# A decoder block in one kernel: the first row's queries, keys and first scores in front of the second row's work, the output weights split on GpSimd, and the statistics of the other rows further on

## The chip, the cores and the metric

One core of one Trainium2 chip runs the whole kernel. The metric is the time of one execution on the device in microseconds (us); lower is better. TensorE (PE) multiplies and transposes, VectorE (DVE) and ScalarE (ACT) work on PSUM and SBUF, GpSimd (POOL) works on SBUF alone, and SyncE (SP) only issues transfers. Every engine runs its own instruction list strictly in order; semaphores join the lists.

## The reference

`x` is 8 rows (batch entries) of 128 tokens by 512 features. Three blocks follow each other, each with a residual: self-attention, cross-attention to a context, and a linear layer with 4-bit weights. The change touches only the self-attention, cut here to what matters:

```python
x = x + _L0_attn_ref(_layernorm(x), Wq, Wk, Wv, Wo)       # changed part
x = x + _L0_xattn_ref(_layernorm(x), ctx_4096, ...)        # most of the time
x = x + _L0_ffn_ref(_layernorm(x), weight_q4, weight_scale, bias)

def _L0_attn_ref(h, Wq, Wk, Wv, Wo):                       # H=32 heads of 16, 8 key heads
    q, k, v = heads(h @ Wq.T), heads(h @ Wk.T), heads(h @ Wv.T)
    qr, kr = apply_rope(q, cos, sin), apply_rope(k, cos, sin)
    scores = einsum('bhqd,bhkd->bhqk', qr, kr) / 4 + causal_mask
    return einsum('bhqk,bhkd->bhqd', softmax(scores), v) @ Wo.T
```

## The kernel before

**Precision.** Products run on fp32 data split in two: a high part, rounded to the matmul format by a copy, and a low part, which is the rest. A product is three matmuls (high·high, low·high, high·low), `split_matmuls`, line 69. So each operand costs a copy (mostly ACT) and a subtraction (DVE or POOL).

**Rows.** The self-attention handles the 8 rows one by one; row n's work is overlapped with the preparation of rows n+1 and n+2. Four hand-written instruction lists, one per engine, have the form of a loop over `n` from -1 (the prologue) on. Nothing is scheduled by a planner: the order in the code is the order on the engine. Lines with `if n == -1` are the prologue.

**A row's steps.**
- `statistics` (DVE, lines 658 and 661) and `rstd_1` (POOL, 329 and 331) give mean and inverse deviation, `normalised` (DVE, 544) the normalised row, `xn_transposed` (PE, 777) its transpose, `xn_high` (ACT, 435) and `xn_low` (DVE, 549) the two parts.
- The projections (PE, line 74) give queries and keys/values. For row 1 the query projection is `second_row_queries`, two halves of six matmuls into `a_ps_o`, placed by hand in the prologue.
- `rope_queries` and `rope_keys` (DVE, 559 to 561) and `rotate_queries` and `rotate_keys` (POOL, 359 to 370) rotate them; `queries_high` (ACT, 442) and `queries_low` (DVE, 593) split the queries. Row 0's queries go in two halves of 16 heads.
- `query_tiles` and `key_tiles` transpose on PE (818, 827) and copy out (ACT 447 and 452, DVE 600).
- `scores(n, k)` for six units k (PE, 842 to 849) alternates between two PSUM banks, `ps_kv` and `ps_q`; `maxima` (DVE, 605), `exps` (ACT, 461), `probs_transposed` (PE 860, copied out by DVE 611) follow. `scores(n, k)` needs the exponentials of unit k-2.
- `inverse_totals` (DVE, 615 and 618) turns the softmax sums into a wide tile that PE transposes (904); `values` (PE, 876 and 884) and `project_output` (PE, line 74 into `a_ps_w`) close the row.

**Output weights.** `a_wo` is loaded into `raw_qo`; ACT makes the high part (line 495), POOL the low part (line 400). The first user is `project_output(0)`.

The cross-attention begins when all engines are through with the self-attention.

Of the kernel before, what the change touches and what calls it, by code (L numbers as in the profile page):

```python
# [28 lines left out]
G = H // KVH  # L29
# [162 lines left out]
def self_attention(nc, mem, io):  # L192
# [12 lines left out]
    with ExitStack() as ctx:  # L205
# [114 lines left out]
        def _(pool):  # L320
# [74 lines left out]
            rstd_1(2, slice(2, 4))  # L395

            def output_weights_low():
# [8 lines left out]
            for m in range(1, B + 2):  # L406
                if m < B:
                    rotate_keys(m)
                if m == 1:
                    rstd_1(3, slice(4, 6))  # L410
                if m < B:
                    rotate_queries(m)
                if m <= B:
                    if m < B:
                        pool.wait_ge(q_lo, m + 2)
                    context(m - 1)
                if m == 1:
                    output_weights_low()
                    rstd_1(4, slice(6, B))
# [12 lines left out]
        def _(act):  # L432
# [56 lines left out]
            for n in range(-1, B + 1):  # L489
                now, after = 0 <= n < B, n + 1 < B  # L490
                if n == -1:
                    xn_high(1)
                    queries_high(0, 0)
                    act.wait_ge(wo_in, 16)
                    act.activation(wo[0][:], raw_qo[:], ACT.Copy).then_inc(wo_hi, 1)
                    queries_high(0, 1)
                elif after:
                    queries_high(n + 1)
# [6 lines left out]
                if n == -1:  # L505
                    key_tiles(0)
                if after:
                    query_tiles(n + 1, 0)
                if after and now:
                    key_tiles(n + 1)  # L510
# [4 lines left out]
                if n == -1:  # L515
                    exps(0, 0)
# [23 lines left out]
        def _(dve):  # L540
# [137 lines left out]
            statistics(range(1, 2))  # L678
            normalised(1)
            dve.wait_ge(tab_in, 32)  # L680
            for n in range(-1, B + 1):
                now, after, later = 0 <= n < B, n + 1 < B, n + 2 < B
                if n == -1:
                    rope_queries(0, 0)
                    rope_keys(0)
                    xn_low(1)
                    pad_values(0)
                    queries_low(0, 0)
                    rope_queries(0, 1)
                elif after and now and n > 0:  # L690
                    rope_queries(n + 1)
# [16 lines left out]
                if n == -1:  # L708
                    dve.wait_ge(x_in, 16)
                    statistics(range(2, 4))  # L710
                    queries_low(0, 1)
                if after:
# [14 lines left out]
                if n == 0:  # L727
                    statistics(range(6, B))
# [5 lines left out]
                if later:  # L734
                    rope_keys(n + 2)
                if n == -1:
                    pad_values(1)
                    maxima(0, 0)
                    maxima(0, 1)
# [10 lines left out]
                if n == -1:  # L750
                    rope_queries(1)
# [6 lines left out]
                if after:  # L758
                    maxima(n + 1, 2)
                if n == -1:  # L760
                    statistics(range(4, 6))
# [7 lines left out]
        def _(pe):  # L769
# [177 lines left out]
            for i in range(WARM_UP // 4):  # L947
                pe.transpose(ps_s[1][:, 0:P], ident[:], ident[:])
            project_keys_values(1)
            pe.wait_ge(consts, 2)  # L950
            for n in range(-1, B):
# [9 lines left out]
                if after:  # L961
# [4 lines left out]
                if after:  # L966
                    query_tiles(n + 1, 0)
                if n == -1:
                    query_tiles(0, 1)
                    second_row_queries(0)  # L970
                    scores(0, 0)
                    scores(0, 1)
                    second_row_queries(1)
                    query_tiles(0, 2)
# [25 lines left out]
                if later and now:  # L1000
                    project_queries(n + 2)
                if after:
                    scores(n + 1, 2)
# [695 lines left out]
```

## Time and profile before

| | |
|---|---|
| median of 3 runs | 947.81 us (946.51 to 948.13) |
| the profiled execution | 946.93 us |
| its span, first to last instruction | 945.2 us |
| PE busy | 915.2 us, 97% of the span |
| DVE, ACT, POOL busy | 726.0, 607.4, 566.9 us |
| granted TensorE clock, mean | 0.994 of full |
| prologue (until the first scores) | about 22 us |
| self-attention ends on PE | about 190 us |

PE's share is an average over stages. The prologue and the first row look different from the rest, so the question is read there, instruction by instruction. A row of the timeline gives the start, the duration, the engine, the line, what was written and read, and in square brackets how long the engine had been idle and who released it. Consecutive instructions of one engine overlap a little, so an instruction starts up to 0.1 us before its predecessor's row ends.

### The profile page before, as it was taken

The page shows a single profiled execution, that of the slowest core. Times are in us where ns is not written, and L with a number is a line of the kernel's source. Part 1 is how long each engine was busy: PE and PEld are TensorE (multiplying, and loading weights), DVE is VectorE, ACT ScalarE, POOL GpSimd, SP SyncE. Part 2 cuts the span into 40 slices and gives each one's busy share as a digit, 9 for nine tenths or more (in the row PEclk, how much of TensorE's full clock was granted, in tenths as well). Part 3 has the DMA queues.
Part 4 walks back from the last instruction along what each step waited for, and adds up shares of the span by engine and source line. Part 5 has one row for each costly group of instructions (what it writes and reads, how often), then busy time and mean ns, then how long its engine had stood idle before and what let it go on. Part 6 is the DMA issues. An engine that isn't in the chain of part 4 may idle for free.

```text
span 945.2 us, 17557 instructions
## 1 busy us (share of the span) xinstructions
PE 915.2 (97%) x5496; PEld 788.4 (83%) x5504; DVE 726.0 (77%) x1559; ACT 607.4 (64%) x2230; POOL 566.9 (60%) x600
## 2 busy tenths in 40 slices
PE   8899998989999999999999999999999999999987
PEld 7677776778888888888888888888888888888776
DVE  7788888667777777777777777777777777789985
ACT  4788887557566756666666567666755675665540
POOL 7532323349656855685578557646865686468742
PEclk9999999999999999999999999999999999999999
DMA  5000120166665666566557655665566556654431
GB/s 213 12 12 13 24 79 12 34 220 218 208 213 165 194 212 205 156 218 203 177 170 232 207 172 172 224 202 156 180 219 212 164 167 212 217 170 150 141 128 57
DMA packets 101164, 149.84 MB, mean 159 GB/s; under 512 B 11856, under 2 KB 77392, under 8 KB 98896
## 3 DMA queue, kind: packets, MB, share of 16 engines
q1 hardware_dynamic: 101072, 148.71, 49.3%
q8 instruction: 45, 0.74, 0.3%
q14 instruction: 47, 0.39, 0.1%
HBM read 87.85 MB, written 60.82 MB: 157 GB/s over the span
## 4 chain that ended last, share of the span: by engine, by line
PE 69%; DVE 4%; POOL 3%; ACT 2%; DMA 1%; issue 1%; SPq 0%; DVEq 0%; POOLq 0%
PE ps_q L74 17%; PE ps_kv L74 17%; PE ps_y L74 17%; PE ps_s L74 8%; PE ps_o L74 8%; POOL wo_lo L1186 1%; POOL pT_raw L1198 1%; ACT ps_s L1273 1%; PE ps_f L74 1%; DMA raw_wkv<-in_x_wkv 1%; DVE neg_max L1352 0%; DVE p L1364 0%; POOL qT_lo L1191 0%; DVE p_blocks L1368 0%; DVE x L1379 0%
## 5 line engine op out<-in xcount | busy, mean ns | idle before, releaser
L1273 ACT ACTIVATE ps_s<-ps_s,bias,q_rms 128x256 f32<-128x256 f32 x256 | 136.6, 534 | 138.2 <-DVE bias L1356 138.2
L1191 POOL TENSOR_TENSOR qT_lo<-qk_raw,qT_hi 128x512 fp32r<-128x512 f32 x64 | 84.8, 1325 | 201.9 <-ACT qT_hi L1285 201.9
L1198 POOL TENSOR_TENSOR pT_raw<-pT_raw,pT_hi_sb 128x1024 fp32r<-128x1024 f32 x63 | 151.7, 2408 | 6.0 <-ACT pT_hi_sb L1279 5.6
L125 ACT ACTIVATE q_squares<-ps_q 128x128 bf16<-128x128 f32 x256 | 67.4, 277 | 109.7 <-DVE qk_blocks L151 109.7
L74 PE MATMUL ps_y<-wo_hi,oT_hi 128*128 128x512 f32 x252 | 99.7, 395 | 4.0 <-DVE oT_lo L1383 4.0
L74 PE MATMUL ps_q<-wq_hi,xT_hi 128*128 128x512 f32 x256 | 101.3, 396 | 0.7 <-PEq L205 0.7
L74 PE MATMUL ps_q<-wq_lo,xT_hi 128*128 128x512 f32 x256 | 101.5, 396 | 0.0
L1368 DVE STREAM_TRANSPOSE p_blocks<-p 128x512 f32<-128x512 f32 x128 | 91.1, 712 | 13.3
L74 PE MATMUL ps_q<-wq_hi,xT_lo 128*128 128x512 f32 x256 | 101.0, 395 | 0.0
L74 PE MATMUL ps_y<-wo_hi,oT_lo 128*128 128x512 f32 x252 | 99.3, 394 | 0.0
L74 PE MATMUL ps_y<-wo_lo,oT_hi 128*128 128x512 f32 x252 | 99.0, 393 | 0.0
L1379 DVE TENSOR_TENSOR x<-ps_y,x 128x512 f32<-128x512 f32 x64 | 44.2, 690 | 66.2 <-PE ps_y L74 65.4
L1364 DVE TENSOR_TENSOR p<-ps_s,inv 128x512 f32<-128x512 f32 x128 | 88.5, 691 | 4.4
L1352 DVE TENSOR_REDUCE neg_max<-ps_s 128x2 f32<-128x512 f32 x128 | 87.6, 684 | 4.9
L151 DVE STREAM_TRANSPOSE qk_blocks<-ps_q 128x512 f32<-128x512 f32 x64 | 45.8, 715 | 41.2 <-PE ps_q L74 41.1
L74 PE MATMUL ps_s<-kT_hi,qT_hi 128*128 128x256 f32 x256 | 72.6, 284 | 3.2 <-DVE kT_lo L1372 2.2
L74 PE MATMUL ps_s<-kT_hi,qT_lo 128*128 128x256 f32 x256 | 72.7, 284 | 0.0
L74 PE MATMUL ps_s<-kT_lo,qT_hi 128*128 128x256 f32 x256 | 72.6, 284 | 0.0
L74 PE MATMUL ps_kv<-wkv_hi,cT_hi 128*128 128x256 f32 x256 | 72.4, 283 | 0.0
L74 PE MATMUL ps_kv<-wkv_hi,cT_lo 128*128 128x256 f32 x256 | 72.2, 282 | 0.0
L74 PE MATMUL ps_kv<-wkv_hi,xT_lo 128*128 128x256 f32 x256 | 71.9, 281 | 0.0
L74 PE MATMUL ps_kv<-wkv_hi,xT_hi 128*128 128x256 f32 x256 | 71.9, 281 | 0.0
(261 smaller groups left out, 2916.1 us busy)
## 6 DMA issues: line engine op xcount, KB each, us to landing
p_scratch<-p_blocks SPq DMA_DIRECT2D x64, 512.0 KB, 3.0
pT_raw<-p_scratch SPq DMA_DIRECT2D x256, 128.0 KB, 3.0
qk_scratch<-qk_blocks SPq DMA_DIRECT2D x64, 384.0 KB, 3.5
qk_raw<-qk_scratch SPq DMA_DIRECT2D x256, 96.0 KB, 3.0
raw_wq<-in_x_wq SPq DMA_DIRECT2D x8, 1024.0 KB, 7.8
raw_wo<-in_x_wo SPq DMA_DIRECT2D x8, 1024.0 KB, 7.8
raw_wkv<-in_x_wkv SPq DMA_DIRECT2D x8, 512.0 KB, 4.9
ctx_raw<-in_ctxT SPq DMA_DIRECT2D x8, 256.0 KB, 2.6
```

What stands on the lines that cost most here:

```text
L74: mm = pe.matmul(out, lhsT, rhs, start=start and i == 0, stop=stop and i == len(terms) - 1)
L125: i = act.activation(x["q_squares"][:, g, :], x["ps_q"][:, g * XD:(g + 1) * XD], ACT.Square, scale=XD ** -0.5, accum_out=x["q_mean"][:, g: ...
L151: dve.transpose(x["qk_blocks"][:, :, 0:XG, :].rearrange("p j x c -> p x j c"), x["ps_q"][:].rearrange("p (g j r) -> p g j r", g=XG, r=R)). ...
L1186: i = pool.tensor_tensor(w[1][:, c, :], raw[:, c, :], f32(w[0][:, c, :]), ALU.subtract)
L1191: pool.tensor_tensor(qT[1][:].rearrange("p g (i c) -> p g i c", i=4), qk_raw[s % 2][:, :, 0:XG, :].rearrange("p i g c -> p g i c"), f32(qT ...
L1198: pool.tensor_tensor(raw, f32(raw), f32(pT_hi_sb[:].rearrange("p i t x -> p (i t x)")), ALU.subtract).then_inc(pT_lo, 1)
L1273: e = act.activation(scores, scores, ACT.Exp, bias=bias[:, g:g + 1], scale=q_rms[:, s % 4, g:g + 1], accum_out=total[:, g:g + 1])
L1352: dve.tensor_reduce(neg_max[:, two], ps_s[h][:].rearrange("p (g k) -> p g k", g=2), AX.X, ALU.max, negate=True).then_inc(max_ok, 1)
L1364: dve.tensor_tensor(p[:, two, :], ps_s[h][:].rearrange("p (g k) -> p g k", g=2), inv[:, two].unsqueeze(2).broadcast_to([P, 2, KV]), ALU.mu ...
L1368: dve.transpose(p_blocks[:, :, two, :], p[:, two, :].rearrange("p g (m r) -> p m g r", r=R)).then_inc(p_blocked, 1)
L1379: dve.tensor_tensor(acc[:, b, :], ps_y[:], acc[:, b, :], ALU.add).then_inc(acc_ok, 1)
```

## The change

On every engine the list of the prologue is re-ordered, and one step moves to another engine:

- **PE**: row 0's query tiles 0 and 1 and its key tiles go in front of row 1's key/value projection, and `scores(0, 0)` and `scores(0, 1)` right behind it. Query tile 2 and `scores(0, 2)` now stand in front of the second half of row 1's queries.
- **DVE**: row 0's first query half is rotated before row 1 is normalised; its values and query low parts come before `xn_low(1)`; key tiles and maxima follow at once. The statistics of rows 2 and 3 move behind `rope_queries(1)`, those of rows 4 and 5 from the prologue into row 0, next to those of rows 6 and 7, ahead of `inverse_totals(0)`.
- **ACT**: `queries_high(0, 0)` before `xn_high(1)`, key tiles before the second query tile, and the output weights' copy is gone.
- **POOL**: `rstd_1` of rows 2 and 3 stands behind `rotate_queries(1)`, that of rows 4 and 5 behind the output weights, of which POOL now does the high part too, in four copies.

```diff
 # POOL
+            def output_weights():
+                pool.wait_ge(wo_in, 16)
+                for g in range(G):
+                    i = pool.tensor_copy(wo[0][:, g, :], raw_qo[:, g, :])
+                i.then_inc(wo_hi, 1)
                 pool.wait_ge(wo_hi, 1)
                 for g in range(G):
                     i = pool.tensor_tensor(wo[1][:, g, :], raw_qo[:, g, :], f32(wo[0][:, g, :]), ALU.subtract)
...
-                if m == 1:
-                    rstd_1(3, slice(4, 6))
                 if m < B:
                     rotate_queries(m)
+                if m == 1:
+                    rstd_1(2, slice(2, 4))
 # ACT
                 if n == -1:
+                    queries_high(0, 0)
                     xn_high(1)
-                    queries_high(0, 0)
-                    act.wait_ge(wo_in, 16)
-                    act.activation(wo[0][:], raw_qo[:], ACT.Copy).then_inc(wo_hi, 1)
-                    queries_high(0, 1)
 # DVE
                 if n == 0:
+                    statistics(range(4, 6))
                     statistics(range(6, B))
                 if now:
                     inverse_totals(n)
 # PE
+            query_tiles(0, 0)
+            query_tiles(0, 1)
+            key_tiles(0)
             project_keys_values(1)
             pe.wait_ge(consts, 2)
+            scores(0, 0)
+            scores(0, 1)
+            second_row_queries(0)
+            query_tiles(0, 2)
+            scores(0, 2)
+            second_row_queries(1)
```

**PE, from the first scores on.** In these rows `a_ps_o` is the projection of row 1's queries, `ps_kv` and `ps_q` the scores of row 0. Before:

```order
L847 MATMUL ps_kv<-a_kT,a_qT 128x256 x2
L849 MATMUL ps_kv<-mask,ident 128x4x64
L847 MATMUL ps_q<-a_kT,a_qT 128x256 x2
L849 MATMUL ps_q<-mask,ident 128x4x64
L74 MATMUL a_ps_o<-wq_hi,a_xnT_hi 128x512
...
L74 MATMUL a_ps_o<-wq_hi,a_xnT_lo 128x512
L818 MATMUL a_ps_u<-ident,q_stack 128x2x64 x4
L842 MATMUL ps_kv<-a_kT,a_qT 128x128 x4
L844 MATMUL ps_kv<-mask,ident 128x512
L818 MATMUL a_ps_t<-ident,q_stack 128x2x64 x4
L860 MATMUL a_ps_pT<-ident,a_p 128x128 x8
```

And with the change, from query tile 2 (`a_ps_u`) on:

```order
L816 MATMUL a_ps_u<-ident,q_stack 128x2x64 x4
L840 MATMUL ps_kv<-a_kT,a_qT 128x128 x4
L842 MATMUL ps_kv<-mask,ident 128x512
L74 MATMUL a_ps_o<-wq_hi,a_xnT_hi 128x512
...
L74 MATMUL a_ps_o<-wq_hi,a_xnT_lo 128x512
L816 MATMUL a_ps_t<-ident,q_stack 128x2x64 x4
L858 MATMUL a_ps_pT<-ident,a_p 128x128 x8
```

The second half of row 1's queries has gone behind the third unit of scores (four small matmuls and the mask), which waits for the exponentials of unit 0.

**DVE, from the third maxima of row 0 to its fourth.** Here `ps_kv` and `ps_q` are units 2 and 3, and `a_ps_o` is row 1's queries. Before:

```order
L559 TENSOR_TENSOR rot_c<-a_ps_o,cos 128x512
L560 TENSOR_TENSOR rot_s<-a_ps_o,sin 128x32x8
L561 TENSOR_TENSOR rot_s<-a_ps_o,sin 128x32x8
L605 TENSOR_REDUCE a_neg_max<-ps_kv 128x8
L658 BN_STATS a_stats<-x 128x6 x2
L661 BN_AGGR a_moments<-a_stats 128x2 x2
L605 TENSOR_REDUCE a_neg_max<-ps_q 128x4
```

With the change:

```order
L604 TENSOR_REDUCE a_neg_max<-ps_kv 128x8
L558 TENSOR_TENSOR rot_c<-a_ps_o,cos 128x512
L559 TENSOR_TENSOR rot_s<-a_ps_o,sin 128x32x8
L560 TENSOR_TENSOR rot_s<-a_ps_o,sin 128x32x8
L657 BN_STATS a_stats<-x 128x6 x2
L660 BN_AGGR a_moments<-a_stats 128x2 x2
L604 TENSOR_REDUCE a_neg_max<-ps_q 128x4
```

The rotation now comes after the third maxima. A pair of statistics still stands in front of the fourth, but it is that of rows 2 and 3, which before was done in the prologue.

**DVE, the end of row 0**, from its key cast for row 1 to the wide inverse; with the change:

```order
L599 CAST a_kT<-a_ps_w 64x4x128
L604 TENSOR_REDUCE a_neg_max<-ps_q 128x8
L610 COPY a_pT<-a_ps_pT 128x512 x2
L657 BN_STATS a_stats<-x 128x6 x2
L660 BN_AGGR a_moments<-a_stats 128x2 x2
L657 BN_STATS a_stats<-x 128x6 x2
L660 BN_AGGR a_moments<-a_stats 128x2 x2
L614 RECIPROCAL a_inv<-a_total 128x32
L617 COPY a_inv_wide<-a_inv 128x512
```

Before, the same list had one pair of statistics here; now it has two.

## Rows read from the trace of the kernel before

**Rows 1.** The page: PE's and DVE's busy time over the whole span

```profile
PE 915.2 (97%) x5496; PEld 788.4 (83%) x5504; DVE 726.0 (77%) x1559; ACT 607.4 (64%) x2230; POOL 566.9 (60%) x600
```

**Rows 2.** Busy time in three stretches: length, engines (instructions), PE clock, DMA

```profile
26.00:29.60 3.60, 1.68 (x14) 1.21 (x11) 3.57 (x8) 3.52 (x21) 1.44 (x3) 1.00 0.00 0
29.60:33.00 3.40, 3.30 (x14) 2.94 (x15) 3.25 (x5) 2.61 (x10) 0.98 (x2) 0.51 0.00 0
60.00:80.00 20.00, 19.13 (x141) 15.46 (x142) 17.32 (x36) 16.85 (x76) 5.89 (x8) 1.00 0.05 14
```

**Rows 3.** Timeline of PE: start, duration, what; idle time before and releaser

```profile
18.59 0.63 PE L827 MATMUL a_ps_w<-ident,k_stack 128*128 128x128 f32 x4 [0.18 <-issue]
...
21.59 0.47 PE L847 MATMUL ps_kv<-a_kT,a_qT 128*128 128x256 f32 x2
...
22.30 0.48 PE L74 MATMUL a_ps_o<-wq_hi,a_xnT_hi 128*128 128x512 f32 x1
...
23.55 0.39 PE L74 MATMUL a_ps_o<-wq_hi,a_xnT_lo 128*128 128x512 f32 x1
...
24.92 0.63 PE L842 MATMUL ps_kv<-a_kT,a_qT 128*128 128x128 f32 x4 [0.54 <-ACT a_p L461]
25.62 0.60 PE L818 MATMUL a_ps_t<-ident,q_stack 128*128 128x128 f32 x4
...
29.66 0.75 PE L847 MATMUL ps_kv<-a_kT,a_qT 128*128 128x256 f32 x2 [1.93 <-ACT a_p L461]
...
30.69 1.12 PE L777 MATMUL a_ps_t<-ident,a_xn 128*128 128x128 f32 x4
...
41.53 0.63 PE L904 MATMUL a_ps_u<-ident,a_inv_wide 128*128 128x128 f32 x4
...
48.37 0.48 PE L74 MATMUL a_ps_w<-a_wo_hi,a_oT_hi 128*128 128x512 f32 x1
```

**Rows 4.** Timeline of DVE

```profile
13.99 0.55 DVE L544 TENSOR_SCALAR a_xn<-x,a_moments,a_rstd 128x512 f32<-128x512 f32 x1 [1.01 <-POOL a_rstd L331]
...
15.19 0.28 DVE L559 TENSOR_TENSOR rot_c<-a_ps_w,cos 128x128 f32<-128x128 f32 x1
...
23.98 0.69 DVE L559 TENSOR_TENSOR rot_c<-a_ps_o,cos 128x512 f32<-128x512 f32 x1 [0.15 <-PE a_ps_o L74]
...
24.92 0.42 DVE L561 TENSOR_TENSOR rot_s<-a_ps_o,sin 128x256 f32<-128x256 f32 x1
...
29.68 0.96 DVE L544 TENSOR_SCALAR a_xn<-x,a_moments,a_rstd 128x512 f32<-128x512 f32 x1
...
36.62 0.68 DVE L600 CAST a_kT<-a_ps_w 64x512 fp32r<-64x512 f32 x1 [2.56 <-ACT a_kT L452]
...
39.02 1.27 DVE L658 BATCH_NORM_STATS2 a_stats<-x 128x6 f32<-128x512 f32 x2
...
40.48 0.32 DVE L615 RECIPROCAL a_inv<-a_total 128x32 f32<-128x32 f32 x1
40.84 0.43 DVE L618 COPY a_inv_wide<-a_inv 128x512 f32<-128x512 f32 x1
```

**Rows 5.** Timeline of ACT

```profile
16.65 1.90 ACT L495 ACTIVATE a_wo_hi<-raw_wq 128x2048 fp32r<-128x2048 f32 x1
...
30.39 1.06 ACT L442 ACTIVATE q_stack<-rot 128x1024 fp32r<-128x1024 f32 x1 [0.87 <-POOL rot L359]
...
35.53 0.59 ACT L452 ACTIVATE a_kT<-a_ps_w 64x512 fp32r<-64x512 f32 x1
```

**Rows 6.** Timeline of POOL

```profile
17.33 1.16 POOL L370 TENSOR_TENSOR k_stack<-rot,k_stack 128x256 fp32r<-128x256 f32 x1
...
29.08 1.27 POOL L359 TENSOR_TENSOR rot<-rot_c,rot_s 128x512 f32<-128x512 f32 x1
32.77 0.61 POOL L383 CAST cT_hi<-ctx_raw 128x512 fp32r<-128x512 f32 x1 [2.42 <-DVE q_stack L593]
...
34.72 5.00 POOL L400 TENSOR_TENSOR a_wo_lo<-raw_wq,a_wo_hi 128x512 fp32r<-128x512 f32 x4
```

More of the change, by code:

```diff
@@ L417, in _ @@
                 if m == 1:
-                    output_weights_low()
+                    output_weights()
+                    rstd_1(3, slice(4, 6))
                     rstd_1(4, slice(6, B))
@@ L504, in _ @@
                     exps(n, 4)
-                if n == -1:
-                    key_tiles(0)
                 if after:
                     query_tiles(n + 1, 0)
-                if after and now:
                     key_tiles(n + 1)
@@ L515, in _ @@
                 if n == -1:
+                    queries_high(0, 1)
                     exps(0, 0)
@@ L678, in _ @@
             statistics(range(1, 2))
+            dve.wait_ge(tab_in, 32)
+            rope_queries(0, 0)
             normalised(1)
-            dve.wait_ge(tab_in, 32)
             for n in range(-1, B + 1):
@@ L683, in _ @@
                 if n == -1:
-                    rope_queries(0, 0)
                     rope_keys(0)
-                    xn_low(1)
                     pad_values(0)
                     queries_low(0, 0)
+                    xn_low(1)
                     rope_queries(0, 1)
+                    key_tiles(0)
+                    maxima(0, 0)
+                    queries_low(0, 1)
+                    maxima(0, 1)
+                    rope_keys(1)
+                    pad_values(1)
+                    maxima(0, 2)
+                    rope_queries(1)
+                    dve.wait_ge(x_in, 16)
+                    statistics(range(2, 4))
                 elif after and now and n > 0:
@@ L707, in _ @@
                     xn_low(n + 2)
[L708 to L712, printed above, removed]
+                if after and now:
                     key_tiles(n + 1)
@@ L733, in _ @@
                     cross_weights_high(0)
-                if later:
+                if later and now:
                     rope_keys(n + 2)
[L736 to L739, printed above, removed]
                 if after and now:
@@ L757, in _ @@
                     step_queries_blocked(dve, mem, 0)
-                if after:
+                if after and now:
                     maxima(n + 1, 2)
-                if n == -1:
-                    statistics(range(4, 6))
                 if n == B - 2:
@@ L960, in _ @@
                     probs_transposed(n, 2)
-                if after:
+                if after and now:
                     key_tiles(n + 1)
@@ L965, in _ @@
                     probs_transposed(n, 3)
-                if after:
+                if after and now:
                     query_tiles(n + 1, 0)
[L968 to L974, printed above, removed]
                 if now:
@@ L1001, in _ @@
                     project_queries(n + 2)
+                if after and now:
+                    scores(n + 1, 2)
                 if after:
-                    scores(n + 1, 2)
                     query_tiles(n + 1, 3)
```

5 lines of the change are left out of this document (1 added, 4 removed).

## The prediction, made before the changed kernel had run

> **What bounds the kernel now.** I read the page first: PE is busy for 915.2 of 945.2 us [rows 1]. A change in the first 45 us therefore acts by one thing: how much earlier or later PE enters the stretch that it then works through. Next the table of stretches. From 60 to 80 us PE works 19.13 of 20.00 us [rows 2], so in the steady rows it is nearly continuous, and a shift at their entry goes on to the end almost one for one. Between 26.0 and 29.6 us it works only 1.68 of 3.60 us, and in the following 3.40 us it is granted 0.51 of its clock, the level of 1.2 GHz instead of 2.4, while busy for 3.30 us [rows 2]. Last, the timelines. The reader should look for the places where PE waits on the way to the steady stretch: 1.93 us in front of unit 4 of row 0's scores, for exponentials [rows 3]; and for where the chain leaves PE. That is the end of row 0: PE's transpose of the wide inverse starts at 41.53, 0.26 us after DVE finished that tile at 40.84 + 0.43 = 41.27 [rows 3, 4]. From there on PE is at work without a long gap. So the forecast is the new time of one instruction, the end of `a_inv_wide` on DVE, against 41.27.
>
> **Step 1, the first scores, a gain.** DVE waited 1.01 us in front of row 1's normalisation [rows 4]; row 0's first query rotation now fills that hole. The key rotation, which began at 15.19, follows the normalisation directly (13.99 + 0.55 less some overlap, 14.5), 0.7 us earlier. POOL's last key part took 1.16 us [rows 6] and ended at 18.49; moved, it ends 0.7 us earlier, or 1.1 if it also loses what stretched it. Row 1's twelve key/value matmuls no longer stand ahead, so the key transposes go from 18.59 [rows 3] to 17.4 to 17.9. Then come the transposes (0.63), ACT's copy (0.59 [rows 5]), DVE's cast (0.68 [rows 4]) and three hand-overs of about 0.1: 2.2 us. First scores at 19.6 to 20.1 instead of 21.59 [rows 3], 1.5 to 2.0 us earlier. The twelve matmuls lie beside that chain.
>
> ACT's removed copy (1.90 us [rows 5]) helps row 0's second query half here, and nothing else waits for it.
>
> **Step 2, row 1's queries, a loss.** Unit 2 of the scores started at 24.92 after waiting for exponentials [rows 3]. It moves with step 1, and by 0.3 us more because DVE takes up the first maxima at once: 22.6 to 23.1. The second half of row 1's queries used to run from 22.30 to 23.94 (23.55 + 0.39), inside that wait [rows 3]. Now it is queued behind the waiting unit 2: 0.70 us for the unit (24.92 to 25.62) and 1.64 for the half, so the queries are ready at 24.95 to 25.45, 1.0 to 1.5 us **later**. Who waits for them: `rope_queries(1)`, and in DVE's order everything behind it.
>
> **Step 3, DVE until row 2 is normalised.** The rotation took 1.36 us (23.98 to 24.92 + 0.42 [rows 4]), 1.28 before the next starts. Behind it now stands a pair of statistics, 1.46 us (39.02 to 40.48 [rows 4]), then maxima and two copies. For these I take the stretch from the key cast at 36.62 to 39.02, 2.40 us, less the cast's 0.60: 1.80. Start of the normalisation: 25.0 to 25.5, plus 1.28 + 1.46 + 1.80 = 4.54, so 29.5 to 30.0. Before it took 0.96 us from 29.68, while POOL was rotating from 29.08 on [rows 4, 6]; the same operation took 0.55 at 13.99 [rows 4]. POOL is now done by then, so it ends at 30.05 to 30.55 instead of 30.64, and PE's transposes of row 2 start 0.1 to 0.6 us earlier than 30.69 [rows 3]. Of the 1.5 to 2.0 us this is what is left. `rotate_queries(1)` is itself much earlier: POOL no longer holds it until 29.08 behind rows 4 and 5's statistics, so `queries_high(1)` leaves 30.39 [rows 5] by some 2 us. That is off the path, because PE and DVE in order come to their part of it no sooner.
>
> **Step 4, PE's clock.** Before, PE went from the 30.69 transposes to row 1's key tiles at 0.51 clock until 33.0 [rows 2, 3]. With the change its wait in front of unit 4 remains, and a second one, until the normalisation, follows it: in the 3 us ahead of the transposes PE works 0.7 us, less than the 1.68 in 3.60 that preceded the fall before. I expect the fall again, chance 7 in 10. Then the key cast at 36.62 [rows 4] comes at 36.0 to 36.5. It began 0.50 us after ACT's copy had ended (35.53 + 0.59 = 36.12 [rows 5]), which is several times the usual hand-over; if that vanishes, 35.5. So 35.5 to 36.5. Without the fall, half of 30.69 to 33.0 is saved, 1.15 us: 34.4 to 35.4.
>
> **Step 5, the statistics at the end of row 0, a loss.** From the cast, DVE does 2.40 us of maxima and copies, then now two pairs of statistics, 2.92 instead of 1.46, then 0.79 until the wide inverse ends (40.48 to 41.27) [rows 4]: 6.11 in all. Before, the single pair ended just as the sums came. Now the second pair lies bare. The inverse ends at cast + 6.11: 41.6 to 42.6 with the slow stretch, middle 42.1, against 41.27: **0.35 to 1.35 us later**, middle 0.85. Without it 40.5 to 41.5: 0.75 earlier to 0.25 later.
>
> **Step 6, output weights on POOL.** Four casts at 0.61 (a 128x512 cast [rows 6]) are 2.4 us, the low parts 5.00 as before. They started at 34.72, after q-parts of row 1 that come up to 0.5 us earlier now; so they end at 41.6 to 42.2. The first user is PE at 48.37 [rows 3]: 6 us of cover, and nothing on the path. The casts would have to take 2.1 us each before PE waited. What they do is keep POOL busy while DVE makes the wide inverse, a copy within SBUF like the normalisation that went from 0.55 to 0.96 beside POOL: between 0 and 0.4 us on the path. I take 0.1, because POOL may just be through. The later `rstd_1` of rows 4 and 5 delays `rotate_keys(2)` on POOL by about 1 us; its tiles are wanted at some 52 us, so it costs nothing.
>
> The Trainium skill (GPSIMD Engine Reference, section Specifications) says that GpSimd shares its SBUF interfaces with VectorE, with contention for VectorE's two-port modes and for its instructions with two SBUF inputs. By that rule the full 0.4 would be paid; by the row at 40.84, where POOL was free, nothing.
>
> **Sum.** 0.85 + 0.1, rounded to 0.9 us later. Against the profiled execution: span 945.2 + 0.9 = 946.1, and 946.93 + 0.9 = 947.8 with what lies around it. That execution was 0.88 us under the median of the runs shown, so for the median 947.81 + 0.9 = 948.7. About 0.2% (1.9 us) is what a measurement of this kernel can tell from no change, so my answer is: none that can be told.
>
> **The rivals.**
> - *Given back, as above*: +0.0 to +1.9, 948.7 (its own range 947.8 to 949.7). Chance 0.50.
> - *Full clock*: the statistics still lie bare, but PE isn't slowed: -0.75 to +0.65, about 947.8. For it: step 2 puts the query half late, near the wait, and the clock may hold. Chance 0.22.
> - *The gain goes through*: steps 2 and 5 cost nothing, because DVE's 2.56 us of waiting in front of the key cast [rows 4] moves with everything else and leaves room. Then the 1.5 to 2.0 us stay: 946.0. Against it: both pairs are listed behind the cast, not in that hole. Chance 0.13.
> - *Slower*: the clock falls a stretch earlier, at PE's wait for unit 2 or 4, and stays down for a second 3.4 us; PE's work in it costs half as much again in wall time, up to 1.7 us on top: 947.81 + 0.9 + 1.7 = 950.4. It decides if the granted clock is already at half before unit 3's scores. Chance 0.10.
> - *Output weights late*: PE would wait at 48.4 for the low part. It needs 6 us more than worked out. Chance 0.03.
> - The rest, 0.02, is what I don't see.
>
> **How the numbers follow.** The likeliest case gives 948.7. The range takes in the full-clock case, most of the gain that goes through, and the lower half of the slower case: 946.0 to 950.2, with some 0.05 left out below and 0.1 above. Faster by over 0.2% (under 945.9) is only the better part of the third case: 0.09. Slower by over 0.2% (above 949.7) is the fourth, half of the fifth and the tail of the first: 0.14. Between them 0.77.
>
> **What would show it.** In the profile after: first scores at 19.6 to 20.1; unit 2 at about 22.9; `rope_queries(1)` starting at 25.0 to 25.5; a granted clock near 0.5 somewhere between 29 and 34; DVE's four statistics of rows 4 to 7 in one piece, with the reciprocal right behind them and the exponentials of row 0 already done; PE idle for about a microsecond in front of the inverse's transposes, which start at 41.0 to 42.9. The prediction is wrong if DVE reaches the reciprocal before 39, if the clock falls twice, or if PE waits for `a_wo_lo`.

## The result and the profile after

| | before | after |
|---|---|---|
| median, timed alternately on one chip | 947.85 us (946.51 to 948.85, 9 runs) | 949.51 us (947.72 to 951.96, 9 runs) |
| the profiled execution, its span | 946.93, 945.2 | 949.63, 947.9 |
| granted TensorE clock, mean | 0.994 | 0.993 |

The ratio is 1.0022 with a 95% interval of 1.0014 to 1.0031: about 2 us slower, 1.66 by the medians, where 0.9 was forecast. On PE the end of row 0 is 0.90 us late, which is the forecast amount; another 1.5 us are lost right behind it, in a stretch at the lower clock that the forecast had at another place.

The page, PE's and DVE's busy time, answers to [rows 1]. The work is the same but for the step that moved (four instructions more on POOL, one fewer on ACT), so what was lost is waiting or work at a lower clock:

```profile
PE 915.4 (97%) x5496; PEld 788.3 (83%) x5504; DVE 726.8 (77%) x1559; ACT 605.6 (64%) x2229; POOL 567.8 (60%) x604
```

The table of stretches after, columns as in [rows 2], with one stretch more:

```profile
26.00:29.60 3.60, 1.68 (x16) 1.47 (x14) 3.57 (x9) 3.18 (x18) 1.88 (x3) 1.00 0.00 0
29.60:33.00 3.40, 2.44 (x20) 2.21 (x21) 3.40 (x6) 3.35 (x15) 0.48 (x2) 1.00 0.00 0
42.00:47.00 5.00, 4.57 (x22) 2.49 (x23) 3.71 (x11) 3.07 (x13) 3.94 (x8) 0.66 0.00 2
60.00:80.00 20.00, 19.14 (x142) 15.47 (x142) 17.36 (x35) 16.84 (x78) 5.89 (x8) 1.00 0.05 17
```

From 29.6 to 33.0 us the clock is full where it was 0.51 [rows 2]. From 42 to 47 us it is 0.66, and PE there issues 22 matmuls. In the kernel before it issued 33 at full clock:

```profile
42.00:47.00 5.00, 4.93 (x33) 3.50 (x33) 3.46 (x11) 4.02 (x18) 1.88 (x3) 1.00 0.01 3
```

PE's timeline after, beside [rows 3]:

```profile
20.68 0.47 PE L845 MATMUL ps_kv<-a_kT,a_qT 128*128 128x256 f32 x2 [0.25 <-DVE a_kT L599]
...
23.68 0.63 PE L840 MATMUL ps_kv<-a_kT,a_qT 128*128 128x128 f32 x4 [0.22 <-ACT a_p L465]
...
25.55 0.39 PE L74 MATMUL a_ps_o<-wq_hi,a_xnT_lo 128*128 128x512 f32 x1
25.78 0.60 PE L816 MATMUL a_ps_t<-ident,q_stack 128*128 128x128 f32 x4
...
29.54 0.47 PE L845 MATMUL ps_kv<-a_kT,a_qT 128*128 128x256 f32 x2 [1.92 <-ACT a_p L465]
...
31.09 0.66 PE L775 MATMUL a_ps_t<-ident,a_xn 128*128 128x128 f32 x4 [0.96 <-DVE a_xn L543]
...
40.15 0.28 PE L847 MATMUL ps_q<-mask,ident 128*128 128x256 bf16 x1
42.43 0.70 PE L902 MATMUL a_ps_u<-ident,a_inv_wide 128*128 128x128 f32 x4 [2.00 <-DVE a_inv_wide L617]
43.05 1.08 PE L874 MATMUL a_ps_o<-a_pT,a_v_pad 128*32 128x256 f32 x8
```

The first scores start 0.91 us earlier than at 21.59. Unit 4 is only 0.12 us earlier than at 29.66, and the inverse's transposes are 0.90 us later than at 41.53 [rows 3]. In the kernel before, PE came to these transposes straight from its own work, and the eight small matmuls behind them, which take 1.08 us now, took 0.64 at full clock:

```profile
41.30 0.28 PE L849 MATMUL ps_q<-mask,ident 128*128 128x256 bf16 x1
...
42.09 0.64 PE L876 MATMUL a_ps_o<-a_pT,a_v_pad 128*32 128x256 f32 x8
```

DVE's timeline after, beside [rows 4]:

```profile
14.02 0.94 DVE L543 TENSOR_SCALAR a_xn<-x,a_moments,a_rstd 128x512 f32<-128x512 f32 x1 [0.28 <-POOL a_rstd L331]
...
16.00 1.19 DVE L592 TENSOR_TENSOR q_stack<-rot,q_stack 128x512 fp32r<-128x512 f32 x1
...
25.98 0.69 DVE L558 TENSOR_TENSOR rot_c<-a_ps_o,cos 128x512 f32<-128x512 f32 x1 [0.70 <-PE a_ps_o L74]
...
30.50 0.54 DVE L543 TENSOR_SCALAR a_xn<-x,a_moments,a_rstd 128x512 f32<-128x512 f32 x1
...
35.48 0.68 DVE L599 CAST a_kT<-a_ps_w 64x512 fp32r<-64x512 f32 x1 [1.51 <-ACT a_kT L456]
...
39.34 1.25 DVE L657 BATCH_NORM_STATS2 a_stats<-x 128x6 f32<-128x512 f32 x2
...
40.80 0.32 DVE L614 RECIPROCAL a_inv<-a_total 128x32 f32<-128x32 f32 x1
41.15 1.22 DVE L617 COPY a_inv_wide<-a_inv 128x512 f32<-128x512 f32 x1
```

The wide copy took 1.22 us instead of 0.43 [rows 4]. What ran beside it stands on POOL's timeline after:

```profile
13.95 0.72 POOL L359 TENSOR_TENSOR rot<-rot_c,rot_s 128x256 f32<-128x256 f32 x1
...
34.76 2.28 POOL L399 CAST a_wo_hi<-raw_wq 128x512 fp32r<-128x512 f32 x4
37.12 4.97 POOL L403 TENSOR_TENSOR a_wo_lo<-raw_wq,a_wo_hi 128x512 fp32r<-128x512 f32 x4
```

The low parts ran until 42.09, beside most of the wide copy. The first row shows POOL rotating beside the normalisation at 14.02.

### The profile page after: what moved, and what is told of

Read it like the earlier page. It is cut to its first block, busy times and chain, and to the rows that moved or that the text cites. A ratio compares the mean times of both kernels' runs of the same rounds, so it can differ in the third digit from the quotient of the medians.

```text
span 947.9 us, 17561 instructions
## 1 busy us (share of the span) xinstructions
PE 915.4 (97%) x5496; PEld 788.3 (83%) x5504; DVE 726.8 (77%) x1559; ACT 605.6 (64%) x2229; POOL 567.8 (60%) x604
## 4 chain that ended last, share of the span: by engine, by line
PE 69%; DVE 4%; POOL 3%; ACT 2%; issue 1%; DMA 1%; SPq 0%; DVEq 0%; POOLq 0%
PE ps_q L74 17%; PE ps_kv L74 17%; PE ps_y L74 17%; PE ps_s L74 8%; PE ps_o L74 8%; POOL wo_lo L1187 1%; POOL pT_raw L1199 1%; ACT ps_s L1274 1%; PE ps_f L74 1%; DMA raw_wkv<-in_x_wkv 1%; DVE neg_max L1353 0%; DVE p L1365 0%; POOL qT_lo L1192 0%; DVE p_blocks L1369 0%; DVE x L1380 0%
```

## Where the time went, by position on PE

A later part of the kernel, which only the filler of e7, e8 and e12 touches, scatters by itself (last column: 749.5 to 753.9 us). The clock falls there too, but that alone isn't the scatter: e2 and e6, with one fall each, differ by 2 us. So total times alone resolve about 0.1%. The profiles resolve more. This table, worked out from the timelines and spans, gives for each profiled execution the start of the inverse's transposes of row 0, the start of the cross-attention on PE, and the length of each fall of the clock in the first 50 us. The last column is the span less the start of the cross-attention.

| kernel | transposes | cross-attention | falls before 50 us | rest |
|---|---|---|---|---|
| before | 41.53 | 194.49 | 3.4 us at 29.7 | 750.7 |
| before again (e10) | 41.27 | 194.35 | none | 749.8 |
| after | 42.43 | 197.41 | 3.4 us at 42.9 | 750.5 |
| after again (e9) | 44.64 | 198.01 | 6.8 us at 30.5 | 750.8 |
| e1, after, statistics in the hole | 41.14 | 194.07 | none | 751.0 |
| e2, after, high part on ACT | 41.69 | 194.57 | none | 752.6 |
| e3, after, query half in front | 44.51 | 197.79 | 6.8 us at 30.0 | 753.9 |
| e4, after, filler at the last wait | 43.57 | 196.48 | 3.4 us at 31.8 | 749.5 |
| e5, before, weights on GpSimd | 42.42 | 195.37 | 3.4 us at 29.6 | 752.4 |
| e6, before, statistics late | 42.39 | 195.43 | 3.4 us at 30.2 | 750.6 |
| e11, before, both | 42.54 | 195.63 | 3.4 us at 30.9 | 750.6 |
| e7, e1 and filler | 41.21 | 193.31 | none | 750.1 |
| e8, before and filler | 42.06 | 195.47 | none | 751.4 |
| e12, e7 and high part on ACT | 40.76 | 192.88 | none | 750.7 |

The same kernel also starts at slightly different times: row 1's normalisation began at 13.99 before, 13.85 in e10 and 14.69 in e8, whose code is the same up to there, and at 14.02 after and 14.32 in e9. That much, up to 0.8 us, is no effect of the code.

From the transposes to the cross-attention the changed kernel loses 2.0 us more (2.92 against 0.90). 1.51 of them lie before the next row's transposes, behind the fall at 42.9. The other 0.5 come later, where the fall in row 6, 3.4 us long at about 159 before, is 6.8 us long at about 162 after.

## The experiments

My theory after the first comparison was this. Two things at the end of row 0 lose the time: the second pair of statistics, and what POOL's work beside it takes from the wide copy (called the port here; the runs show its price and not the port itself). The clock's fall at 42.9 us follows from the 2.00 us wait that they make. The rivals were that the late query half on PE does it (step 2), that the statistics alone do it, and that the difference is only scatter of the clock. Three batches were run. Within each, every kernel was timed alternately with the kernel before; its median was 947.73, 949.12 and 947.49 us, so medians of different batches are not compared.

### e1, the statistics of rows 4 and 5 in DVE's hole

```diff
 # DVE, the changed kernel
                 if later and now:
                     xn_low(n + 2)
+                if n == 0:
+                    statistics(range(4, 6))
...
                 if n == 0:
-                    statistics(range(4, 6))
                     statistics(range(6, B))
```

> The changed kernel with one edit: the statistics of rows 4 and 5 are taken from in front of the reciprocal of row 0 and put in front of the key cast for row 1, where VectorE stands idle for 1.51 us in the changed kernel's trace. Theory A (the wide inverse on VectorE sets when TensorE goes on): the reciprocal comes at about 39.4 instead of 40.80, the wide copy still takes about 1.2 us beside GpSimd's low parts and ends near 41.0, TensorE waits about 0.6 instead of 2.00 us there, so 1.4 us less; if the granted clock then holds from 43 to 46 us, another 1.5 us less. Time 1.4 to 2.9 us under the changed kernel: 946.6 to 948.1. Theory B (the loss comes from row 1's queries being projected late, the statistics are covered): no change from 949.5.

Measured: 948.31 us (946.56 to 950.43; 946.6 to 948.1 expected), ratio 1.0006 (0.9995 to 1.0017), so no loss can be told any more, though the interval still touches that of the changed kernel (1.0014 to 1.0031). On DVE the statistics are now ahead of the key cast, and the cast starts 0.32 us later than at 35.48:

```profile
33.80 1.27 DVE L657 BATCH_NORM_STATS2 a_stats<-x 128x6 f32<-128x512 f32 x2
...
35.80 0.68 DVE L599 CAST a_kT<-a_ps_w 64x512 fp32r<-64x512 f32 x1 [0.45 <-ACT a_kT L456]
...
39.67 0.32 DVE L614 RECIPROCAL a_inv<-a_total 128x32 f32<-128x32 f32 x1
40.02 1.06 DVE L617 COPY a_inv_wide<-a_inv 128x512 f32<-128x512 f32 x1
```

The reciprocal is 1.13 us earlier. On PE the wait in front of the transposes shrinks from 2.00 to 0.39 us, and in this execution no fall followed it:

```profile
41.14 0.66 PE L903 MATMUL a_ps_u<-ident,a_inv_wide 128*128 128x128 f32 x4 [0.39 <-DVE a_inv_wide L617]
```

### e2, the high part of the output weights on ACT again

The four casts leave POOL and ACT's one copy stands where it stood, behind `xn_high(1)`.

```diff
 # ACT
                     xn_high(1)
+                    act.wait_ge(wo_in, 16)
+                    act.activation(wo[0][:], raw_qo[:], ACT.Copy).then_inc(wo_hi, 1)
```

> The changed kernel with one edit: the high part of the output weights is made by ScalarE again, in one copy behind the split of row 1's normalised row; GpSimd only makes the low part. Theory A with the port: GpSimd's low parts end near 39.8 instead of 42.1, so the wide copy takes 0.43 instead of 1.22 us and TensorE's wait of 2.00 us shrinks by 0.8; with a clock that holds, 1.5 us more. Time 947.2 to 948.7. Rival (the wide copy is long for another reason, or moving the copy back to ScalarE costs as much in the prologue): wide copy still over 1 us, or time within 0.3 us of 949.5.

Measured: 950.33 us (948.36 to 953.35), ratio 1.0032 (1.0018 to 1.0047). POOL was through by 39.81, the wide copy took 0.43 us again (it began at 41.21), and the transposes started at 41.69, 0.74 us earlier than in the changed kernel. The port's price at this place is thus shown. The total isn't lower, against the expectation of 947.2 to 948.7: this profile enters the cross-attention at 194.57, as before, and spends 752.6 us behind it. Why its timed runs are as long as those of the changed kernel is not settled. It is clear only that the extra time of the profiled one lies in a part that this edit doesn't touch.

### e3, the second query half in front of unit 2

```diff
 # PE
             second_row_queries(0)
+            second_row_queries(1)
             query_tiles(0, 2)
             scores(0, 2)
-            second_row_queries(1)
```

> The changed kernel with one edit: the second half of row 1's queries stands in front of query tile 2 and unit 2 of row 0's scores again, as before the change. Theory A: the rotation of row 1's queries on VectorE starts about 0.9 us earlier (at 25.1 instead of 25.98, behind unit 2's maxima, which come about 1 us later than now), and everything in order behind it moves by 0.3 to 0.9 us: the wide inverse ends at 41.5 to 42.1. Time 948.6 to 949.2, or 947.1 if the clock holds. Theory B (late queries are the whole loss): the inverse comes back to 41.3 and the time to 947.9. If unit 2's delay costs as much as the earlier queries give: no change.

Measured: 950.15 us (947.24 to 953.46), ratio 1.0025 (1.0015 to 1.0036), no better and above the expected 948.6 to 949.2; the profiled execution (953.46) was the slowest of its twelve. ACT's timeline shows why: its copy of query tile 2 waits for PE and stands ahead of the exponentials of unit 1.

```profile
25.00 0.60 ACT L451 ACTIVATE a_qT<-a_ps_u 128x512 fp32r<-128x512 f32 x1 [1.37 <-PE a_ps_u L816]
```

On DVE the rotation, which could have gone ahead, started at 26.25, later than the 25.98 of the changed kernel. It stands behind the maxima of unit 2, and these now waited 1.33 us for PE. So step 2's loss can't be mended by moving the half on PE alone: it moves from DVE's wait to ACT's.

### e4, filler transposes in front of the inverse's

```diff
 # PE
+                if n == 0:
+                    pe.wait_ge(qT_sb, 7)
+                    for i in range(14):
+                        pe.transpose(ps_u[:, 0:P], ident[:], ident[:])
                 if now:
                     inverse_transposed(n)
```

> The changed kernel with work added and nothing taken away: 14 transposes of the identity into the PSUM bank that the inverse's transposes then overwrite, placed where TensorE waits 2.00 us for the wide inverse of row 0. Theory A: the inverse is ready at 42.4 as before and the filler (14 x 0.11 = 1.6 us) lies inside the wait; TensorE's granted clock stays at full through 43 to 46 us and the work there takes 1.5 us less. Time 948.0. Rival (the clock at 43 to 46 us isn't what costs, or has nothing to do with the wait): time 949.5 or, if the filler runs over, up to 950.5.

Measured: 947.88 us (947.17 to 950.31), ratio 1.0005 (0.9994 to 1.0016). The median is the expected one, but this profile doesn't show the expected reason. The clock had already fallen at 31.8, ahead of the filler, and stayed full behind it, so whether the filler prevents the fall at 42.9 is not seen here. By the timed runs it takes out some fall: the mean granted clock was 0.996 or more in nine of the eleven, and 0.995 or less in each of the fifteen runs of the changed kernel (nine, and six in e9). The loss is within the interval gone although both suspects are still in place, so a good part of it seems to hang on the clock. The profile does show what an early fall costs the changed kernel. Its key cast:

```profile
37.16 0.68 DVE L599 CAST a_kT<-a_ps_w 64x512 fp32r<-64x512 f32 x1 [3.16 <-ACT a_kT L456]
```

That is 1.68 us later than at full clock (35.48). By then POOL is through, so the wide copy took 0.43 us, and the transposes, at 43.57, are only 1.14 us later than the 42.43 of the changed kernel. Part of that is the filler itself, which ran 0.3 us beyond the end of the wide copy.

### e5, e6 and e11: the two suspects put into the kernel before

e5 takes the kernel before, gives POOL the four casts and takes the copy from ACT. e6 moves the statistics of rows 4 and 5 to the end of row 0, ahead of the reciprocal, and their `rstd_1` on POOL behind the output weights. e11 does both. None of them touches the order of the first scores.

```diff
 # DVE, the kernel before (e6, e11)
                 if n == 0:
+                    statistics(range(4, 6))
                     statistics(range(6, B))
...
-                if n == -1:
-                    statistics(range(4, 6))
 # POOL (e5, e11)
+                for g in range(G):
+                    i = pool.tensor_copy(wo[0][:, g, :], raw_qo[:, g, :])
+                i.then_inc(wo_hi, 1)
```

> The kernel before with one part of the change alone: GpSimd makes the high part of the output weights too, in four casts in front of the low parts; ScalarE's copy is gone. Theory A with the port: the low parts end near 42.1 instead of 39.7, so the wide copy of row 0 (40.84, 0.43 us) takes about 1.2 us, PE's transposes of it go from 41.53 to about 42.3, 0.8 us later, and the time is 948.5, more where the granted clock falls behind the new wait of 0.9 us. Rival (the port costs only where two statistics pairs had made VectorE late): time 947.7, wide copy 0.43.

> The kernel before with another part alone: the statistics of rows 4 and 5 go from the prologue's end to the end of row 0, in front of those of rows 6 and 7, and GpSimd's part of them behind the output weights. Theory A: two things against each other. The prologue loses 1.46 us of VectorE and a wait on GpSimd, so row 1's queries are ready about 1.5 us earlier and the key cast at 36.62 comes up to 1 us earlier; in front of the reciprocal VectorE does 1.46 us more. Net 0.5 to 1.5 us later: 948.2 to 949.2. Rival (the statistics are covered by the exponentials): 947.0, because only the gain is left.

> The kernel before with the output weights wholly on GpSimd and the statistics of rows 4 and 5 late, without any of the re-ordering of the first scores. By the theory that the change lost 1.1 us through these two at the end of row 0: reciprocal at about 41.5 and the wide copy at 0.43 to 1.3, according to whether POOL is through by then; transposes at 42.4 to 43.2, so 0.9 to 1.7 us over the kernel before, ratio 1.001 to 1.002. By the rival that only the clock's falls set the measured time: no difference to the kernel before that can be told, 0.999 to 1.001.

Measured: e5 948.14 us, ratio 0.9988 (0.9973 to 1.0003); e6 947.84 us, 0.9991 (0.9979 to 1.0003); e11 948.16 us, 1.0012 (1.0003 to 1.0022). The times of e5 and e6 tell no loss, and that of e11, though it is the expected 1.001 to 1.002, hardly more than the kernel before shows against itself (e10). So the timed runs don't show that a delay of this size at the transposes reaches the end. Their profiles show the delay. In e5 the wide copy beside POOL:

```profile
40.86 1.51 DVE L620 COPY a_inv_wide<-a_inv 128x512 f32<-128x512 f32 x1
```

And in e6 the second pair of statistics, with the reciprocal 1.07 us later than at 40.48 [rows 4]:

```profile
40.10 1.25 DVE L657 BATCH_NORM_STATS2 a_stats<-x 128x6 f32<-128x512 f32 x2
41.39 0.25 DVE L660 BATCH_NORM_AGGREGATE a_moments<-a_stats 128x2 f32<-128x6 f32 x2
41.55 0.32 DVE L614 RECIPROCAL a_inv<-a_total 128x32 f32<-128x32 f32 x1
```

Each alone delays the transposes by 0.9 us (42.42 and 42.39 against 41.53), and both together only by 1.0 (42.54). In e11 the statistics push the wide copy to 42.06, when POOL is through (its low parts ended at 41.66), and it took 0.43 us. So the two prices don't add up: where one is paid, it carries DVE past the other. The changed kernel pays both, because its key cast comes 1.1 us earlier than before and brings the copy back beside POOL. In e5, e6 and e11 PE waited 0.83, 1.20 and 1.20 us for the wide copy, and no fall followed there; each had the early one.

### e9 and e10, the two kernels themselves once more

> The changed kernel itself, unchanged, beside the kernel before: it says how far a ratio moves from one batch to the next. If the statistics and the port each cost what their rows say, the ratio comes again between 1.001 and 1.003. If the loss of 0.2% was chance, the ratio is between 0.999 and 1.001. Its profile should again show the wide inverse at about 1.1 to 1.5 us on DVE beside POOL's low parts, and its transposes at about 42.4.

> The kernel before, under a second name, against itself: a ratio of 1 within 0.001 by every theory. If it comes out further from 1 than that, differences of 0.1% between the other runs must not be read.

Measured: after 949.55 us (948.86 to 951.55), ratio 1.0024 (1.0011 to 1.0037); before against itself 947.90 us, ratio 1.0007 (0.9997 to 1.0016). The loss repeats, and a tenth of a per cent is what the same kernel shows against itself. What I had not expected is the profile of e9, where the wide copy took 0.43 us and the transposes started at 44.64, not the expected 1.1 to 1.5 us and 42.4. The stretches:

```profile
29.60:33.00 3.40, 2.19 (x11) 1.99 (x12) 3.40 (x6) 2.89 (x12) 0.64 (x1) 0.63 0.00 0
33.00:37.00 4.00, 4.00 (x19) 3.53 (x17) 1.37 (x3) 1.68 (x9) 3.77 (x6) 0.50 0.20 52
```

This execution of the same changed kernel has the fall that the prediction expected, twice as long. DVE's key cast then waits 3.78 us and comes 3.00 us later than in the first profile (35.48), of which 0.30 us are the later start. The wide copy begins when POOL is long through (42.41):

```profile
38.48 0.68 DVE L599 CAST a_kT<-a_ps_w 64x512 fp32r<-64x512 f32 x1 [3.78 <-ACT a_kT L456]
...
44.16 0.43 DVE L617 COPY a_inv_wide<-a_inv 128x512 f32<-128x512 f32 x1
```

The kernel before hardly feels it. e10 had no early fall, and PE's and DVE's timelines there show:

```profile
32.86 0.63 PE L842 MATMUL ps_q<-a_kT,a_qT 128*128 128x128 f32 x4 [0.76 <-ACT a_p L461]
...
36.36 0.68 DVE L600 CAST a_kT<-a_ps_w 64x512 fp32r<-64x512 f32 x1 [2.43 <-ACT a_kT L452]
```

The key cast at full clock came at 36.36, with the fall at 36.62 [rows 4], and e10 began 0.1 us earlier. PE at full clock waits 0.76 us for exponentials; at half clock it arrives just as they are ready. In the changed kernel ACT's `queries_high(1)` and with it these exponentials are a microsecond earlier, that wait is gone, and PE's clock lies bare. With the start of each execution taken off, the key cast is 0.1 us later in the kernel before, and in the changed one 1.65 us for a fall of 3.4 us (e4) and 2.70 for one of 6.8 (e9).

### e7, e8 and e12: filler in the waits, and the port once more

The filler is 12 transposes of the identity in front of unit 4 and 6 in front of row 2's transposes in row 0, 18 in row 6 and 18 in front of the second cross-attention step. They write PSUM banks that are free at that point. e7 has it on top of e1, e8 on the kernel before, e12 on top of e1 and e2.

```diff
 # PE, one of the places
+                if n == 0:
+                    for i in range(12):
+                        pe.transpose(ps_w[:, 0:P], ident[:], ident[:])
                 if now:
                     scores(n, 4)
```

> The changed kernel with the statistics of rows 4 and 5 in VectorE's hole in front of the key cast (as in the first experiment) and with filler, transposes of the identity into banks that are free, at four waits of TensorE: 12 in front of unit 4 of row 0 (wait 1.92 us), 6 in front of row 2's transposes (0.96), 18 in front of the last unit's transposes of row 6 (2.23), 18 in front of the second step's scores of the cross-attention (2.20). The filler fits each wait at 0.11 us a piece, so it takes no time itself. Theory A (clock falls behind such waits cost 1 to 1.7 us each where TensorE is the bound): mean granted clock 0.998 or more, time 945.3 to 946.5, below both kernels. Rival (the falls lie in waits anyhow): the same as the first experiment, 948.3.

> The kernel before with the same filler at the same four waits, and nothing else changed. Theory A: mean granted clock 0.998 or more and time 945.7 to 946.7; the difference to the run with the changed front and the statistics in the hole is what the re-ordered prologue itself is worth, 0.4 us by the transposes of the wide inverse in the two traces (41.53 and 41.14). Rival: 947.7, unchanged.

> The changed kernel with the statistics of rows 4 and 5 in the hole in front of the key cast, the high part of the output weights on ACT again, and the filler transposes in the four waits. If the port cost is on the path, the wide copy takes 0.43 instead of 1.07 and the transposes start at about 40.6 instead of 41.2: about 0.6 us below the same kernel with the weights on GpSimd, so a ratio of 0.995 to 0.997. If PE at that point waits for something else (the exponentials of row 0, PE's own work), the ratio stays at about 0.997.

Measured: e7 945.98 us (945.17 to 948.46), ratio 0.9969 (0.9959 to 0.9979); e8 947.24 us (945.54 to 948.69), 0.9973 (0.9963 to 0.9983); e12 945.74 us, ratio 0.9991 (0.9978 to 1.0004), where one run of 952.02 widens the interval and the other ten lie between 944.78 and 947.75; by its ratio e12 shows no gain, where 0.995 to 0.997 was expected. e7 came out as expected and is faster than both kernels, and its profile has no fall of the clock at all. But e8 gains nearly as much without any of the change, though its median is 0.5 us above the expected 945.7 to 946.7. Its profile kept two falls of 3.4 us, at about 165 in row 6, behind a wait of 1.61 us that the filler there doesn't cover, and at about 913, where no filler stands. The timed runs show the clock: 1.000 in eight of twelve runs of e7 and in five of twelve of e8, while no run of the kernel before was above 0.998 in any of the three batches. At a clock of 1.000 the medians are 945.70 us for e7 and 945.87 for e8, so what is gained is the clock, and the order of the first row is worth 0.2 us or less. Two stretches, row 6 and the start of the cross-attention, in e1 and then in e7 (its matmuls include the filler):

```profile
155.00:165.00 10.00, 7.28 (x48) 4.69 (x46) 8.82 (x16) 7.49 (x34) 5.09 (x5) 0.83 0.11 28
204.00:212.00 8.00, 5.20 (x30) 5.03 (x30) 7.42 (x18) 5.38 (x24) 4.91 (x7) 0.79 0.83 290
```

```profile
155.00:165.00 10.00, 8.05 (x68) 6.10 (x66) 9.63 (x18) 8.15 (x38) 5.04 (x5) 1.00 0.07 26
204.00:212.00 8.00, 8.00 (x60) 7.54 (x59) 7.24 (x18) 5.14 (x24) 4.81 (x8) 1.00 0.68 216
```

The port is seen once more in the wide copy, e7 and then e12:

```profile
40.09 1.07 DVE L617 COPY a_inv_wide<-a_inv 128x512 f32<-128x512 f32 x1
```

```profile
40.06 0.43 DVE L615 COPY a_inv_wide<-a_inv 128x512 f32<-128x512 f32 x1
```

The copy ends 0.67 us earlier, but the transposes start only 0.45 earlier (40.76 against 41.21): PE is then itself at work until there, on the scores of row 1's unit 1. They still stand as 0.43 us at the cross-attention (192.88 against 193.31) and are too small for the timed runs.

## Why the prediction was right and where it was not

The forecast, about 0.9 us later by the inverse's end and no gain, had the right sign and the right place. The measured loss of 1.7 us in the medians (949.51 against 947.85) lies inside the range and at the upper edge of the likeliest case's own. The answer "none that can be told" was too weak: nine runs of each tell the difference, and e9 tells it again. And that PE came to the transposes 0.90 us late, the very amount forecast, is partly luck: the fall of the clock that the 0.9 counted on wasn't in that execution, and a smaller gain in step 1 and a dearer wide copy made up for it.

- **Step 1, the gain of the first scores, was mis-sized**: 0.91 us instead of 1.5 to 2.0. I had moved the normalisation and the rotations to their new places at their old durations. With the change POOL already rotates the first query half while DVE normalises: 0.94 instead of 0.55 us [rows 4], and the low query parts at 16.00 took 1.19 us, against 0.69 for the same operation in the kernel before. Which of the two starts first seems to matter too: at 17.19 before, DVE's 0.69 us began ahead of POOL's `k_stack` at 17.33, and it was POOL's that grew, to 1.16 us from the 0.73 it took at 25.09 after. POOL's last key part did end at 17.78, as forecast, but PE's key transposes began only at 18.40: two query tiles stand in front of them, and the second could start only at 17.94, when DVE's `xn_low(1)`, itself pushed back by those long instructions, had read the bank `a_ps_t` (17.11 + 0.68).
- **Step 2, row 1's queries late, held** in its cause. The rotation started at 25.98, not at 25.0 to 25.5, because unit 2 itself came later. I missed its second victim. ACT's copy of the fourth query tile waits for PE, whose transposes (25.78) stand behind that same half, and ahead of unit 2's exponentials. ACT's timeline after:

```profile
26.42 0.60 ACT L451 ACTIVATE a_qT<-a_ps_t 128x512 fp32r<-128x512 f32 x1 [0.92 <-PE a_ps_t L816]
26.92 0.32 ACT L465 ACTIVATE a_p<-ps_kv,a_neg_max 128x64 f32<-128x64 f32 x1
```

  Before, the same two started at 26.51 and 26.98. The exponentials of unit 0 were still 1.23 us ahead (22.04 against 23.27); here the gain is gone, and unit 4 stands where it stood.
- **Step 3 held in its length, not in its result**: from the rotation at 25.98 to the normalisation at 30.50 are 4.52 us (4.54 summed), and that took 0.54 us again. But it ended at 31.04, later than my 30.05 to 30.55 by what step 1 was short, and PE's transposes started at 31.09, 0.4 us later than before instead of earlier.
- **Step 4, the clock, failed as put.** I gave 7 in 10 to a fall at 30 us. The first profile has none there, the second (e9) has one of 6.8 us, and its 950.57 us are near those of the rival "Slower", 950.4. I also priced the full-clock case as "half of 30.69 to 33.0 is saved" from the kernel before; e10 shows that the fall cost that kernel almost nothing, since a wait of 0.76 us covered it. The key cast at full clock came at 35.48, not at 34.4 to 35.4.
- **Step 5, the bare statistics, held to the letter**: from the cast at 35.48 to the reciprocal at 40.80 are 5.32 us, as summed. e6 (+1.07) and e1 (-1.13) show the pair's price from both sides.
- **Step 6, output weights, was mis-sized.** The casts took 2.28 us, the low part ended at 42.09 and its first user on PE came at 51.1, so the cover was as forecast. But the wide copy cost 0.79 us more, where I had 0 to 0.4 and took 0.1. I had bounded it by the normalisation, which overlapped POOL for only part of its time. Three pairs that differ in this step alone show that POOL's work is the cause: after and e2 (1.22 and 0.43), e7 and e12 (1.07 and 0.43), e5 and before (1.51 and 0.43).
- **The sum.** The inverse ended at 42.37, 1.10 us late, and PE's transposes came 0.90 late. I had taken the 0.26 us between 41.27 and 41.53 for the way from the tile to PE. It was PE's own work, which ended there (the rows at 41.30 above); after, PE started 0.06 us behind the tile. The same rows show what was thrown away: PE's work ahead of the transposes was done 1.15 us earlier than before (40.15 against 41.30), and it then waited 2.00 us. The rest came from what I had not on the list: behind that wait the clock fell for 3.4 us in work that has no slack. The next row's transposes came 21.25 us later (63.68 - 42.43), against 19.74 before (61.27 - 41.53): 1.51 us more. PE's rows, before and then after:

```profile
61.27 0.60 PE L904 MATMUL a_ps_u<-ident,a_inv_wide 128*128 128x128 f32 x4
```

```profile
63.68 0.60 PE L902 MATMUL a_ps_u<-ident,a_inv_wide 128*128 128x128 f32 x4
```

  In e9, where it fell at 30 instead, the transposes were 3.1 us late and nothing was added.

The Trainium skill (GPSIMD Engine Reference, section Specifications) says that GpSimd and VectorE contend for the shared SBUF interfaces where VectorE runs in a two-port mode or has two SBUF inputs. The trace agrees for the two inputs (0.69 against 1.19 us in step 1); the mode of the wide copy isn't shown, but it was slowed, and the rule's side was the right one to take here: 0.43 against 1.06 to 1.51 us, which is more than the 0.4 us that I had put on that side.

Not settled: whether the 2.00 us wait causes the fall at 42.9, since e1 and e2 (waits of 0.39 and 1.21 us, no fall) agree with it but are one execution each; and why e2 is no faster than the changed kernel. The timed medians hold both the delay and the falls. The granted clocks of e9's batch part them roughly: at 0.994, three runs of the changed kernel have a median of 948.97 us and fifteen of the kernel before 947.96, so about 1.0 us of the loss stands at equal clock, by an estimate from few runs, and the rest goes with the clock.

## What to carry to other kernels

When an instruction is moved, read its duration from where it will stand: beside which other engine it runs decides it, and perhaps which of the two starts first (one pair of rows here). When a step is put in front of a queue, follow it on every engine whose list holds a consumer; here the late query half took the gain away through ACT's in-order copy, a place where nothing had waited before. And a wait that looks like waste may be what hides a slow stretch: without it, falls of the clock cost 1.65 and 2.70 us at the key cast, where one had cost 0.1.

## What the runs showed of the hardware

- A 128x512 copy on DVE within SBUF took 0.43 us with POOL's engine free and 1.06, 1.07, 1.22 and 1.51 us beside its subtraction of the same width. The maxima, which read PSUM, took 0.67 us beside POOL's work (at 36.09 after, at 37.22 before) and 0.69 at 22.52 after, when POOL was idle. The statistics, which read SBUF, took 1.27 and 1.25 us for two beside POOL (at 37.88 and 39.34 after) and 1.28 without (at 26.43 before).
- The same kernel, executed twice, had its clock fall at different places: 3.4 us at 42.9, and 6.8 us at 30.5. The kernel before fell at 29.7 in one execution and not at all in its first 150 us in another. One profile is not enough to place a fall.
- Useless transposes in four waits of PE took the falls out of e7's and e12's profiled executions and gave 0.3% (e7, e8), more than the whole change had moved. e8's profiled execution kept two.
